# Fewer gathers ahead of the first product of a sorted part, and four other moves in a graph layer on one core

## The reference, cut

```python
xn = layernorm(x)
msgs = weight[:, None] * xn[col]                      # 53125 x 256
h = segment_sum(msgs, row, 3125)                      # graph sum
gnn = h @ gnn_W.T + gnn_b
q, k, v = split(xn @ Wqkv.T); q, k = elu(q) + 1, elu(k) + 1
t = (q @ (k^T v)) / (q . sum(k) + eps)                # linear attention, 8 heads
x1 = layernorm(t + xn) * g1 + b1_
mix = layernorm(gelu(x1 @ W1.T + b1) @ W2.T + b2 + x1) * g2 + b2_
x = x + gnn + mix
z = layernorm(x)                                      # 25 tiles of 128 rows, the last has 53
rw = router(mean(z)); top two of 8 experts, weights w
y = sum_e w_e * (gelu(z @ We1 + be1) @ We2 + be2)
out = x + layernorm(y + z) * g + b
```

## Time and profile before

| | |
|---|---|
| median of 3 runs | 953.44 us (951.49 to 954.23) |
| profiled execution | 949.6 us, its span 947.9 us |
| PE busy | 781.0 us (82%), granted clock 0.932 of full on average |
| PEld busy | 638.3 us (67%) |
| DVE busy | 682.2 us (72%) |
| ACT busy | 415.1 us (44%) |
| POOL busy | 582.3 us (61%) |
| gathers (L707) | 440, 424.3 us busy, 2.8 us from issue to landing (median) |

### The profile page before, as it was taken

One profiled execution on the slowest core, in us unless ns is written; L12 is line 12 of the kernel. 1 busy time (PEld: TensorE's weight loads), 2 busy tenths in 40 slices (PEclk: granted clock), 3 DMA queues, 4 the chain that ended last, 5 costly groups with the idle time before them and its releaser, 6 DMA issues.

```text
span 947.9 us, 14062 instructions
## 1 busy us (share of the span) xinstructions
PE 781.0 (82%) x4353; PEld 638.3 (67%) x4353; DVE 682.2 (72%) x1939; ACT 415.1 (44%) x1008; POOL 582.3 (61%) x648
## 2 busy tenths in 40 slices
PE   7879868888887788878877877768777777999997
PEld 5649866776776456556655656556655646999997
DVE  8889859999887555445555867668676687666676
ACT  2736755675773133313332323222223326666551
POOL 3847578878887577676666666666666610333453
PEclk9998979999899899989997989989898899999999
DMA  7210033233333333334233333233332311000000
GB/s 244 79 61 2 10 98 88 84 91 88 89 87 100 95 96 113 88 92 121 84 108 89 111 90 113 86 90 113 91 112 86 110 32 56 13 23 24 23 30 31
DMA packets 38994, 76.88 MB, mean 81 GB/s; under 512 B 9811, under 2 KB 22536, under 8 KB 38920
## 3 DMA queue, kind: packets, MB, share of 16 engines
q0 software_dynamic: 21120, 57.70, 20.9%
q1 hardware_dynamic: 17800, 18.29, 6.1%
HBM read 69.48 MB, written 6.48 MB: 80 GB/s over the span
## 4 chain that ended last, share of the span: by engine, by line
PE 42%; DVE 12%; issue 8%; POOL 6%; ACT 2%; DVEq 1%; DMA 0%; POOLq 0%
PE bank L2021 14%; PE bank L1812 10%; DVE X L1301 6%; POOL ARENA L707 6%; PE bank L1863 5%; PE bank L1870 2%; DVE ARENA L1289 2%; PE bank L1937 2%; PE bank L1926 2%; PE bank L1878 1%; PE bank L1770 1%; PE bank L1649 1%; PE bank L1940 1%; DVE ST L1033 1%; DVE KS L1351 1%
## 5 line engine op out<-in xcount | busy, mean ns | idle before, releaser
L707 POOL DMA_INDIRECT ARENA<-xg_rows,ARENA x440 | 424.3, 964 | 197.8 <-issue 121.1
L1812 PE MATMUL bank<-ARENA 128*128 128x256 f32 x880 | 246.6, 420 | 90.2 <-issue 43.9
L1301 DVE TENSOR_TENSOR X<-bank,X 128x256 f32 x440 | 185.3, 421 | 182.2 <-PE bank L1812 167.8
L1812 PEld LDWEIGHTS bank<-ARENA 128*128 128x128 f32 x880 | 171.4, 207 | 141.0 <-issue 57.2
L1289 DVE TENSOR_SCALAR ARENA<-iota,ARENA 128x128 f32<-128x128 f32 x440 | 157.7, 363 | 0.0
L1770 PE MATMUL bank<-OIA,ASA 128*128 128x128 f32 x676 | 93.0, 304 | 16.3 <-issue 6.1
L1770 PEld LDWEIGHTS bank<-OIA,ASA 128*128 128x128 f32 x676 | 91.5, 220 | 19.9 <-issue 18.8
L828 ACT ACTIVATE OIA<-iota,LANE 128x128 f32<-128x128 f32 x286 | 85.9, 389 | 13.9 <-PE bank L1770 13.6
L996 ACT ACTIVATE HF<-bank,FB 128x262 f32<-128x262 f32 (+1 forms) x96 | 46.8, 487 | 42.1 <-PE bank L2021 22.6
L872 ACT ACTIVATE NK<-bank 128x256 f32<-128x256 f32 x25 | 9.6, 383 | 116.3 <-PE bank L1863 116.3
L2021 PE MATMUL bank<-QH,W1L 128*128 128x262 f32 (+1 forms) x192 | 55.9, 291 | 2.3 <-DVE W1L L1548 1.7
(11 more groups left out here) (320 smaller groups left out, 1540.6 us busy)
## 6 DMA issues: line engine op xcount, KB each, us to landing
ARENA<-xg_rows,ARENA POOLq DMA_INDIRECT x440, 2.8
FW1A<-in_exp_w SPq DMA_DIRECT2D x8, 512.0 KB, 3.8
xg_rows<-XGS SPq DMA_DIRECT2D x12, 256.0 KB, 2.1
out<-YO SPq DMA_DIRECT2D x24, 128.0 KB, 1.7
X<-in_x SPq DMA_DIRECT2D x1, 1664.0 KB, 12.4
X<-in_x SPq DMA_DIRECT2D x1, 1536.0 KB, 8.1
FW<-in_exp_w SPq DMA_DIRECT2D x2, 512.0 KB, 4.6
QKVW<-in_qkv_wT SPq DMA_DIRECT2D x1, 768.0 KB
```

The costliest lines, as they stand in the source:

```text
L707: pool.indirect_dma_start(RING[:, at, :], None, xg_dram, bass.IndirectOffsetOnAxis(ap=SIX[:, c:c + 1], axis=0)).then_inc(gathered[at // HA ...
L1301: V.tensor_tensor(xt, pair_bank(pair)[:, half * C:(half + 1) * C], xt, ALU.add).then_inc(x_added, 1)
L1812: ins = T.matmul(pair_bank(pair)[:, u * C:(u + 1) * C], SEL[:, t % 2 * HAND + k, :], RING[:, h * HAND + k, :], start=True, stop=True)
```

## The change

Five moves, no instruction's work is altered.

1. `ED_AFTER`: the third piece of `ed` is spread after tile 21, not 23; DVE's reads of the pieces become `piece_columns`, the first of them ahead of the last early rank.
2. GpSimd, second sorted part: in step n gathers up to 2 * upto(n + 1) + min(2n, 4), so 6, 14, 22, 28, ... and 124 at the last step in place of 14, 20, 26, 32, ... and 128; then a wait until gather 123 has landed, and the eight others.
3. The last tile's out-norm and update stand two column pairs sooner on DVE.
4. `AHEAD` is 7 and the order of tiles 0 to 5, 24, 6, 7 and on. Tiles 24 and 6 (`AT_ROUTER`) are turned beside the router; on ACT their norms and those of 7 and 8 come ahead of the router's first exponential, their high parts behind it; on DVE their low parts ahead of all low parts of block 0.
5. On PE they are turned ahead of the router's products of no use, of which there are 3, not 4; tile 24 isn't turned behind block 0's up products any more.

Empty lines and some lines of context are left out of the diff.

```diff
@@ -411,9 +411,9 @@
         BATCHES = ((0, 12), (12, TILES))
-        AHEAD = 8
-
-        EL_AFTER, LB_AFTER, ED_AFTER, BID_AFTER = (16, 16, 18), (17, 17, 19), (19, 20, 23), 24
+        AHEAD = 7
+
+        EL_AFTER, LB_AFTER, ED_AFTER, BID_AFTER = (16, 16, 18), (17, 17, 19), (19, 20, 21), 24
         RANKS_FROM = 12
@@ -424,6 +424,7 @@
         B_PAIRS = 7
+        AHEAD_OF_PAIRS = 4
         B_FIRST = COLS // 2 - 12 - B_PAIRS * PAIRS
@@ -437,7 +438,8 @@
-        TURNS = list(range(AHEAD)) + [TILES - 1] + list(range(AHEAD, TILES - 1))
+        TURNS = list(range(AHEAD - 1)) + [TILES - 1, AHEAD - 1] + list(range(AHEAD, TILES - 1))
+        AT_ROUTER = TURNS[AHEAD - 1:AHEAD + 1]
@@ -716,12 +718,13 @@
             for n in range(LATER):
-                so_far = min(COLS_A, 2 * upto(n + 1) + 8)
+                so_far = 2 * upto(n + 1) + min(2 * n, AHEAD_OF_PAIRS)
                 for c in range(issued, so_far):
...
                     group_columns(GA + n + 1)
+            pool.wait_ge(*landed(issued - 1))
             for c in range(issued, COLS_A):
@@ -970,13 +973,13 @@
             ffn_high(range(2, 6))
-            ffn_normalise(range(6, 8))
+            ffn_normalise(AT_ROUTER)
+            ffn_normalise(with_block(0))
             router_exp(0, NE)
+            ffn_high(AT_ROUTER)
             router_exp(1, NE)
...
             act.activation(R[0:1, 1, 5:6], zeros[0:1, 0:1], ACT.Gelu)
-            ffn_high(range(6, 8))
-            ffn_normalise([TILES - 1])
             act.wait_ge(fb1_ready, 1)
@@ -997,10 +1000,9 @@
             for b in range(NBLK):
-                ffn_normalise(with_block(b))
+                if b:
+                    ffn_normalise(with_block(b))
                 hidden(b, range(NH))
-                if b == 0:
-                    ffn_high([TILES - 1])
                 ffn_high(with_block(b))
@@ -1125,13 +1127,16 @@
             V.tensor_copy(DD[:, :, 0:1], DC[:, SA:SETS, 0:1]).then_inc(dd_ready, 1)
+            def piece_columns(k):
+
+                lo, hi = PIECES[k]
+                dve.wait_ge(lb_ready, k + 1)
+                dve.wait_ge(ed_done, k + 1)
+                V.scalar_tensor_tensor(out=DCB[:, lo:hi], in0=LB[:, lo:hi], scalar=local_p[:, 0:1],
+                                       in1=piece_bank(1, k)[:, 0:hi - lo], op0=ALU.is_le, op1=ALU.mult).then_inc(ed_read, 1)
+
             def group_columns():
-                for k, (lo, hi) in enumerate(PIECES):
-                    dve.wait_ge(lb_ready, k + 1)
-                    dve.wait_ge(ed_done, k + 1)
-                    V.scalar_tensor_tensor(out=DCB[:, lo:hi], in0=LB[:, lo:hi], scalar=local_p[:, 0:1],
-                                           in1=piece_bank(1, k)[:, 0:hi - lo], op0=ALU.is_le, op1=ALU.mult).then_inc(ed_read, 1)
                 dve.wait_ge(ed_read, len(PIECES))
@@ -1247,8 +1252,12 @@
                 V.tensor_scalar(CMP[:, part, :], iota_c[:, :], CBP[:, part:part + 1], None, ALU.is_ge).then_inc(bid_cmp, 1)
-            for g in range(EARLY_RANKS):
+            for g in range(EARLY_RANKS - 1):
                 slot_rank(g)
+            piece_columns(0)
+            slot_rank(EARLY_RANKS - 1)
+            piece_columns(1)
+            piece_columns(2)
             group_columns()
@@ -1465,11 +1474,10 @@
             b_update(PAIRS - 1, (0, 1), p + 8)
-            columns(p + 8, p + 10)
             b_out(PAIRS, (0,))
-            columns(p + 10, p + 11)
-            b_update(PAIRS, (0,), p + 11)
-            columns(p + 11, COLS // 2)
+            columns(p + 8, p + 9)
+            b_update(PAIRS, (0,), p + 9)
+            columns(p + 9, COLS // 2)
@@ -1621,10 +1629,8 @@
-            split_hidden(0, 0, range(0, 4))
-            low_parts(range(6, AHEAD))
-            split_hidden(0, 0, range(4, 8))
-            low_parts([TILES - 1])
+            low_parts(AT_ROUTER)
+            split_hidden(0, 0, range(0, 8))
             scale_w2()
@@ -2011,8 +2017,8 @@
             ins.then_inc(logits_done, 1)
-            stay_busy(bank[4], 4)
-            ffn_transpose(range(6, 8))
+            ffn_transpose(AT_ROUTER)
+            stay_busy(bank[4], 3)
@@ -2062,7 +2068,6 @@
             ups(0, range(FJ, NH))
-            ffn_transpose([TILES - 1])
             ffn_transpose(with_block(0))
```

## The result

The changed kernel takes 949.06 us (median of 9 runs, 944.42 to 951.41) against 954.23 us for the kernel before in the same comparison. The ratio is 0.9949, 95% interval 0.9926 to 0.9971, which is 4.9 us less, between 7.1 and 2.8. The forecast was 947.0 (943.8 to 950.8) from a median of 953.44, or 6.4 less. One of the nine runs of the kernel before took 1358.8 us and does not enter the ratio. The gain is there and the time lies in the range. The profiled executions, however, are nearly equal: the span is 947.5 us where it was 947.9.

A forecast was written before the change was run, and what follows sets the result against it. GpSimd's queue was taken to set the pace for 650 us, with VectorE and TensorE bounding before and TensorE after. Terms -1.97, -0.2, -0.6 and -3.6 sum to -6.4 us: 953.44 to 947.0 us, range 943.8 to 950.8.

The forecast's parts named there:

- (a): Head: third column piece read sooner, so the first gather moves from 114.93 to 112.96; -1.97 us, bounds 0 and -3.2.
- rival 1: Head gains nothing because the bucket product or a tile's evacuation ends last; then -4.4 us, 949.0; chance 0.13.
- (b): GpSimd's queue: reordering 0 us, new wait +1.74, wait ahead of gather 132 -1.97; sum -0.2, bounds +1.7 and -2.0.
- Rival 4: Slower: VectorE paces the second sorted part and makes GpSimd wait; no gain up to 959 us; chance 0.07.
- (c): Last tile: its update leaves the stretch between the last two pairs; -0.6 us, bounds -0.3 and -1.2.
- (d): Router and first blocks: first down product starts at 805.4 to 805.7 instead of 809.32; -3.6 us, bounds -4.5 and -2.0.
- Rival 2: TensorE's clock, halved after idle time before the up products, or the landings take part; -3 to -4.5 us, 950.0; chance 0.17.

The follow-up runs named there:

- all but the queue: The changed kernel with the gather order of the kernel before and without the new wait: 945.83 us against 951.6 for the kernel before, -7.3 us.

## Why the prediction was right, and where not

The four terms were -1.97, -0.2, -0.6 and -3.6.

**(a) Head, right.** 1.95 us in the trace against 1.97. The bucket products were in time, by 0.37 us where I had 0.5, so rival 1 falls by the trace; the runs alone (-1.0, between -2.9 and +1.0) wouldn't have decided it. The first gather starts at 114.6 in the mean of three traces without this edit and at 112.6 in ten with it. The first gather moved by 3.87 because two other things moved with it: the 1.21 us of an earlier start, and 0.7 us in the first group's products (8.16 us for 52, 8.87 before). TensorE had run at 1.2 GHz for 5.9 us of them before and did so for 4.5 us now. The prediction had this as a bound of (a), not in its -1.97.

**(b) Queue, right in its shape, mis-sized by 1.5 us in the runs and by 4 in the traces.** The sum was -0.2. The runs give +1.3 and +1.4, inside the stated bounds of -2.0 and +1.7; the traces give +0.8 up to gather 132 and +2.9 behind it, outside them. Group 13's products started at 124.03, where I had said 126, the second table and the mixing weights' loads came 9 us sooner, and none of this moved the gathers, as said. Three terms were off.
- First, the wait ahead of gather 132, for which I took the normal 2.04 us, was 2.5 to 2.6 in six traces with the new order, and the old one, 4.01 in the earlier trace rows, was 3.2 to 4.0 in six other traces with the old order, 3.5 in the mean. The gain is 1.0 us, not 1.97. With the wait added, gathers 0 to 132 take 198.3 us in the mean of five traces (197.9 to 198.8) against 197.4 in seven with the old order (196.9 to 198.1): +0.8, not -0.2.
- Second, the step "no gather is removed, hence 0 us from the reordering itself" left out what a gather's own length hangs on. The forecast took a gather's mean, 954 ns up to 308.8 us and 969 after it, as a constant. The 15 ns more, times 308, are 4.6 us: six gathers that the additions of loop A held (5.4 us over 0.95 each). How many of 13 are held depends on how the two queues lie against each other. With the old order it was six or seven (four traces), with the new seven, nine, nine and nine (four traces), and together 5.4 to 6.6 us against 6.8 to 8.7.
- Third, 132 to last took 449.8 to 452.7 us with the old order and 453.9 to 455.6 with the new, a mean of 2.9 us. The held gathers are 1.9 of it, the landing waits 0.9. With none held it was the other way round, 444.80 with the new order and 446.82 with the old. Four traces against four point to the edit bringing more gathers into the additions, and no more than that; by which step of the two queues it would do so wasn't shown.

The traces also overstate the loss. The profiled executions of the four kernels with the new order took 0.1 to 3.8 us more than their medians, 1.8 in the mean; those of the four with the old order lay 2.0 under to 2.3 over theirs, near 0 in the mean (949.6 of the kernel before against the 951.6 of 29 runs). So 1.5 us or more of the 3.7 between the two orders is which execution was profiled, and the rest agrees with the runs.

The prediction's own test, "Wrong if first to last gather takes over 2 us more than 762.64 - 114.93 = 647.7 us", came out as wrong: 763.64 - 111.06 = 652.6. In the second execution of the changed kernel it was 654.1. The edit's cost to the queue was foretold too small, though the total held. Rival 4 had a sentence on GpSimd and VectorE blocking each other, weighed it only for GpSimd's products, and gave the gathers no price.

**(c) Last tile, right.** From the last gather to the first mean products it took 14.7 us in the mean of four traces without the edit and 13.5 in six with it, -1.2 with the executions' different clocks in it. (The three kernels with fewer landing waits are left out: there TensorE is further behind at the last gather, and it takes 14.9 to 16.0.) Compared at equal length of the last 16 products (5.5 us), 13.76 went to 13.08, 12.97 and 13.20, that is -0.7; at 6.6 us it went from 15.21 to 14.20, -1.0. I had -0.6, bounds -0.3 and -1.2.

**(d) Router and first blocks, right.** From first up product to first down product: 17.61, 17.60 and 17.57 us without the edit, 14.01 to 14.05 in the seven executions with it whose up products start at 2.4 GHz, or -3.6 as worked out, and alone it is -3.3 in the runs. The named successors were right too (block 1's up products without a gap, the transposes waiting 0.53 us for low parts). In the one trace of the change the gain from last gather to the dense products was only 1.5 us, from 46.68 to 45.14, where (c) and (d) had foretold 4.2. Most of the rest is clock: the last pairs 1.2 us and the mean products 1.2 us longer than in the trace before. These mean products took 2.00 us in seven traces and 3.1 to 3.4 in six; one of the long ones has no edit at the router, and five of the short ones have it, so this is not the change's. Rival 2's mechanism exists, at 1.4 us in three of ten executions with the edit; not in the profiled ones of the change. The prediction had expected 2.3 us of idle time there; it is 2.5. What the Trainium skill (TensorE: Matmul & The Clock Gate, "What's actually happening") says of variation from run to run, it says of the way up to full clock. For the way down the evidence here is the ten executions.

**The sum.** Taken one by one in the runs, head -1.0, queue +1.3, router -3.3 and the rest of what "all but the queue" gained, -3.0 for the last tile, add to -6.0; the change gave -4.9 and -5.2. The intervals of the parts are about 2 us to either side, so the -3.0 left for the last tile says less than the -0.7 to -1.0 of the traces. The forecast of -6.4 is 1.2 to 1.5 too much, and +1.3 of the queue against -0.2 would be just that. That the total came out inside the range shows little by itself: the range was wide enough for rivals 1 and 2 as well, and the first profiled execution of the change was only 0.4 us shorter than the one before. What holds the terms up is each one's own rows.

**Left open:** why the landing waits behind gather 132 took 61.3 us over the pause in the mean of four traces with the new order and 60.4 in four with the old, and whether the new order of gathers gains anything once no gather is held; 940.86 against 941.62 can't tell.

## What to carry to other kernels

Where one queue paces a kernel, an edit that takes nothing out of it gives nothing but its own waits, and every wait taken out of it comes back in full until the next engine's first wait appears (here 17 waits gave 32.6 us of the queue): that can be tried at once by halving them. A mean duration that differs between two stretches of the same instruction is a finding, not rounding: look at the longest ones and at what the other engines run at their start. Where GpSimd issues gathers beside VectorE, let VectorE's long additions take one input from PSUM.

## What the runs showed of the hardware

- A gather issued by GpSimd (0.95 us) is held by a VectorE instruction with both inputs in SBUF, `tensor_tensor` as well as `scalar_tensor_tensor`: it ends 0.82 us after the instruction that holds it. With two additions of 0.69 us one behind the other that made up to 2.2 us, with single ones of 128x256 up to 1.21. With one input in PSUM, 18 of 18 gathers beside the same additions took 0.94 or 0.95, and none of 1933 beside `X<-bank,X` over 0.99.
- A wait for the landing of the gather before costs GpSimd's queue 1.74 us by the idle time over the pause of a single one, 1.79 to 1.89 in the mean of the 33 behind gather 132, and 1.9 us by taking 17 of them away.
- The same 26 products of one row took 2.00 us in seven executions and 3.1 to 3.4 in six others. After 2.50 us without work TensorE ran at 1.2 GHz in three executions of ten and at 2.4 GHz in seven; after 1.72 us at 2.4 GHz in three of three.
